# The last attention and the quantised feed-forward in one block, with two kinds of copies moved to VectorE

## The chip, the cores and the metric

The kernel runs on one core of a Trainium2 chip. The metric is the device time of one execution in microseconds (us); the median of the runs counts. The engines of the core are TensorE (products, into the PSUM banks), VectorE, ScalarE, GpSimd and SyncE (SP, which starts most DMA transfers). Each runs its own instruction stream and waits on semaphores.

## The reference, cut to what matters

x has 32 tiles of 128 rows by 256 columns. The program is two layers: an attention and a mixture of experts, then a masked attention and a feed-forward whose operands are quantised. Only the second layer is touched:

```python
x = x + _L1_xattn_ref(_layernorm(x), ctx_1024, ctx_1024, mask_BxS_bk1)
x = x + _L1_ffn_ref(_layernorm(x), L1_ffn_w1, L1_ffn_b1, L1_ffn_w2, L1_ffn_b2)

def rmsnorm(x):
    return x * rsqrt(mean(square(x), -1) + 1e-06)
def activation_quant(x):
    scale = 127.0 / clip(max(abs(x), -1), 1e-5)
    return clip(round(x * scale), -128, 127) / scale
def weight_quant(w):
    scale = 1.0 / clip(mean(abs(w)), 1e-5)
    return clip(round(w * scale), -1, 1) / scale
def bitlinear(x, w, b):
    return einsum('bsi,oi->bso', activation_quant(rmsnorm(x)), weight_quant(w)) + b
# ffn: bitlinear(gelu(bitlinear(x, w1, b1)), w2, b2); w1 is 1024 x 256, w2 256 x 1024
```

## The kernel before, in words

Four blocks run one after the other: `attend0`, `experts`, `attend1` and `bitffn`. A block ends when all engines have ended it. x (`x_rows`) stays in SBUF throughout. The order of work on each engine is written out by hand: an engine's `group(i)` lists eight tiles (R = 8, and Q = 4 is half of that), `at_tile(step, i, k, behind)` places a step so many tiles behind the tile k, and `schedule` runs group 0 written out, groups 1 and 2 as a loop, group 3 (NR - 1) and a last group(NR) for what is behind. In the loop the semaphores are compared with registers.

`attend1` (lines 1016 to 1345) gathers the expert rows (GpSimd), adds them to x and takes the norms (VectorE), turns q, takes scores, turns the exps and multiplies (TensorE, with ScalarE's copies out of PSUM), and adds to x (L1278), whose moments `x_moments` (st3) L1283 takes. It also sums, rounds and signs the feed-forward's weights on ScalarE into the ternary `w1q` and `w2q`. VectorE waits at its beginning for the b1 rows (L1323), and `mean_of` (L1333, L1336) stands before its group(0).

`bitffn` (lines 1348 to 1713), per tile:

- VectorE takes the norms of all 32 tiles at once (`norms`, L113 to L119 and L128 to L138), and only then GpSimd centres the rows (`centre`, L1422) and adds b2 (`add_b2`, L1429).
- `largest_x` (L1571) takes the largest of a centred row, `scale_x` (nine small instructions for four tiles, L1584 to L1602) its scales, GpSimd's `round_x` (L1435) rounds x to `x_rounded` by adding a constant that leaves the whole number in the low half.
- TensorE turns the low halves (`turn_x`, L1497) into PSUM bank 0; ScalarE's `keep_xt` (L1458) copies them, takes the constant off and scales, into `x_whole_T` (bf16). The scales go the same way: `turn_b` (L1507) and VectorE's `keep_b` (L1610).
- `up` (L1517, L1520) multiplies into banks 1 and 2 with b1's parts; ScalarE's `gelu` (L1464) writes `hidden_ffn` (128x1024), `square` (L1473) sums its squares.
- VectorE's `largest_h` (L1614) takes the largest, `scale_h` (17 small instructions for four tiles: L1624, the square root's eleven, L1628 to L1638) the scales, `round_h` (L1644) rounds to `h_rounded`, seven tiles behind `gelu`. The rounding needs the whole chain.
- TensorE's `turn_h` (L1528), ScalarE's `keep_ht` (L1478, 128x1024), TensorE's `down` (L1536), VectorE's `finish` (L1651), eight tiles behind, and SP's store.

TensorE's order of a tile in `bitffn` is `turn_x` of the next, `up`, `down` of eight behind, `turn_h` of seven behind, so `down` of a tile stands directly in front of `turn_h` of the next.

## Time and profile before

| | us |
|---|---|
| median of 3 runs | 780.03 (779.78 to 781.59) |
| the profiled execution | 777.34 |
| its span, first to last instruction | 775.6 |
| VectorE busy | 533.2 (69%) |
| TensorE busy | 556.9 (72%) |
| ScalarE busy | 369.1 (48%) |
| GpSimd busy | 366.1 (47%) |

The busy shares of the whole span mix four stages; the stretch from about 487 us to the end is the second layer, and from 627 us on its feed-forward. In the page and in the rows, PE is TensorE's products and PEld its weight loads, DVE is VectorE, ACT ScalarE, POOL GpSimd. A row of the timeline gives start and duration in us, engine, line, operation, out<-in with shapes, the count, and in brackets how long the engine had been idle before it and what ended that. Instructions of one engine overlap a little at their ends, so the time one costs is read from its start to the start of the next.

### The profile page before, as it was taken

To read this page: it belongs to the slowest core of one execution; us is meant where nothing else is said; L and a number is where in the kernel's file an instruction comes from. 1 tells how busy PE (TensorE), PEld (TensorE's weight loads), DVE (VectorE), ACT (ScalarE), POOL (GpSimd) and SP (SyncE) were. 2 spreads that over 40 slices of the span, in tenths; PEclk is the share of its full clock that TensorE was granted. 3 is DMA by queue.
4 is the path that set the end of the run, shared out by engine and by line. 5 is a ranking of instruction groups with operands and counts; after the bars stand their busy time and mean duration, and the time that the engine had idled before them with its cause. 6 is when DMAs were issued, how large, how long until landed. Compare 5 with 4: busy or idle time off the path is not lost. (4 is left out here: it accounts for less than half of the span.)

```text
span 775.6 us, 18120 instructions
## 1 busy us (share of the span) xinstructions
PE 556.9 (72%) x5883; PEld 484.5 (62%) x5883; DVE 533.2 (69%) x1486; ACT 369.1 (48%) x707; POOL 366.1 (47%) x384
## 2 busy tenths in 40 slices
PE   4787736005999999999999997033656736877774
PEld 3666625005999999999999997022444513555553
DVE  6887655154777766766656564375778878999994
ACT  2598634002343334334334433224534628988883
POOL 1024264747999999995000000475644054455431
PEclk9687855557999999999999999556867969999999
DMA  6996141232222222232222221933544100010011
GB/s 213 344 362 226 59 146 52 104 116 42 61 65 66 61 69 64 63 70 63 63 66 67 64 69 42 305 100 117 164 136 135 55 0 0 29 35 34 31 46 49
DMA packets 77585, 74.76 MB, mean 96 GB/s; under 512 B 44480, under 2 KB 67904, under 8 KB 76224
## 3 DMA queue, kind: packets, MB, share of 16 engines
q1 hardware_dynamic: 71360, 56.92, 23.9%
q0 software_dynamic: 6144, 16.79, 6.7%
q8 instruction: 48, 0.79, 0.4%
q14 instruction: 33, 0.27, 0.1%
HBM read 40.51 MB, written 23.86 MB: 83 GB/s over the span
## 5 line engine op out<-in xcount | busy, mean ns | idle before, releaser
L911 PE MATMUL banks<-z_turned,w_of_block 128*128 128x128 f16 x3408 | 203.8, 220 | 26.5 <-DMA z_turned<-z_rows 26.5
L911 PEld LDWEIGHTS banks<-z_turned,w_of_block 128*128 128x128 f16 x3408 | 191.8, 98 | 29.6 <-DVE w_of_block L984 26.6
L992 DVE SCALAR_TENSOR_TENSOR hidden_T<-banks,blk_inv,silu_T 128x512 f32<-128x512 f32 x71 | 53.3, 751 | 99.3 <-PE banks L911 99.2
L413 POOL DMA_INDIRECT z_rows<-z_parts,places_in_regions x64 | 63.0, 984 | 104.8 <-DVE places_in_regions L719 86.7
L984 DVE COPY w_of_block<-w_parts 128x4096 f16 x71 | 98.2, 1384 | 10.4 <-issue 10.4
L957 ACT ACTIVATE hidden_T_high<-hidden_T 128x512 fp32r<-128x512 f32 x71 | 44.9, 633 | 109.2 <-DVE hidden_T L992 109.2
L924 PE MATMUL banks<-w_low,hidden_T_high 128*128 x284 | 86.0, 303 | 1.5 <-DVE hidden_T_low L998 1.5
L1107 POOL DMA_INDIRECT expert_rows_in<-expert_rows,places_of_rows x64 | 62.5, 977 | 48.2 <-DVE x_rows L1236 26.2
L950 ACT ACTIVATE silu_T<-banks,blk_inv 128x512 f32<-128x512 f32 x71 | 48.8, 688 | 72.3 <-PE banks L911 72.3
L924 PE MATMUL banks<-w_high,hidden_T_low 128*128 x284 | 79.9, 281 | 0.0
L924 PE MATMUL banks<-w_high,hidden_T_high 128*128 x284 | 79.8, 281 | 0.0
L1111 POOL MEMSET ones_ffn<- 128x128 f32 x1 | 0.2, 204 | 124.0 <-POOLq L845 124.0
L879 POOL TENSOR_SCALAR w_parts<-w_parts,w_scale 128x512 f32<-128x512 f32 x24 | 53.3, 2221 | 10.3 <-POOLq L334 7.5
L998 DVE TENSOR_TENSOR hidden_T_low<-hidden_T,hidden_T_high 128x512 fp32r<-128x512 f32 x71 | 56.0, 789 | 1.7 <-ACT hidden_T_high L957 1.7
L1429 POOL TENSOR_TENSOR x_plus_b<-x_rows,b_rows 128x256 f32<-128x256 f32 x32 | 29.6, 926 | 57.1 <-DVE rows_out L1651 57.1
L924 PEld LDWEIGHTS banks<-w_low,hidden_T_high 128*128 128x128 f32 x284 | 53.5, 188 | 2.0 <-issue 2.0
L924 PEld LDWEIGHTS banks<-w_high,hidden_T_high 128*128 128x128 f32 x284 | 53.7, 189 | 0.0
L924 PEld LDWEIGHTS banks<-w_high,hidden_T_low 128*128 128x128 f32 x284 | 53.4, 188 | 0.0
L511 PEld LDWEIGHTS banks<-gate_T,work 128*128 128x128 f32 x128 | 26.3, 274 | 34.3 <-ACT work L461 18.7
L1184 PE MATMUL banks<-ident,q_neg 128*128 128x128 f32 x64 | 17.3, 363 | 41.9 <-ACT q_neg L1125 32.6
L1478 ACT ACTIVATE h_whole_T<-banks,magic 128x1024 bf16<-128x1024 f16 x32 | 35.8, 1119 | 20.4 <-PE banks L1528 20.4
L511 PE MATMUL banks<-gate_T,work 128*128 128x8 f32 x128 | 25.8, 311 | 25.9 <-ACT work L461 14.9
(235 smaller groups left out, 1297.4 us busy)
## 6 DMA issues: line engine op xcount, KB each, us to landing
expert_rows<-expert_out SPq DMA_DIRECT2D x71, 128.0 KB, 1.7
w_parts<-in_w SPq DMA_DIRECT2D x7, 1024.0 KB, 7.1
x_rows<-in_x SPq DMA_DIRECT2D x8, 512.0 KB, 5.7
c_T<-in_ctx_turned SPq DMA_DIRECT2D x16, 256.0 KB
w_low<-in_w SPq DMA_DIRECT2D x8, 512.0 KB, 8.8
c_T_in<-in_ctx_turned SPq DMA_DIRECT2D x32, 128.0 KB
c_in<-in_ctx_rows SPq DMA_DIRECT2D x32, 128.0 KB
out<-rows_out SPq DMA_DIRECT2D x32, 128.0 KB, 1.7
```

The costliest lines, as they stand in the source:

```text
L413: pool.indirect_dma_start(z_rows[:, :], bass.IndirectOffsetOnAxis(ap=put_at[:, t, k:k + 1], axis=0), zp[:, t % ZP, :], None).then_inc(scat ...
L511: mm = pe.matmul(PS[:, 6, (t - t0) * E:(t - t0 + 1) * E], zT[:, t % 2, c * P:(c + 1) * P], gT[:, c, :], start=(c == 0), stop=(c == DC - 1))
L879: ch.link(pool.tensor_scalar(raw[:, cols], raw[:, cols], wsc[:, e:e + 1], None, ALU.mult))
L911: mm = pe.matmul(PS[:, 1 + half + 2 * u, hc * P:(hc + 1) * P], win[:, u, wp, c, at:at + P], zT[:, j % ZB, k, :], start=(n == 0), stop=(n = ...
L924: mm = pe.matmul(PS[:, 6 + u, 0:D], gg[:, u, c * P:(c + 1) * P], w[:, e, c, :].rearrange("p a d -> p (a d)"), start=(n == 0), stop=(n == 3 ...
L950: a.activation(s[:, :], PS[:, 1 + 2 * u, :], ACT.Silu, scale=blk_inv[:, j:j + 1])\
L957: a.activation(gh[:, u, :], g[:, :], ACT.Copy).then_inc(gh_made, 1)
L984: v.tensor_copy(win[:, u, :, :, :].rearrange("p a c h -> p (a c h)"), W12[:, bass.ds(e[j % READ], 1), :, :, :].rearrange("p b a c h -> p ( ...
L992: v.scalar_tensor_tensor(out=g[:, :], in0=PS[:, 2 + 2 * u, :], scalar=blk_inv[:, j:j + 1], in1=s[:, :], op0=ALU.mult, op1=ALU.mult).then_i ...
L998: v.tensor_tensor(gl[:, u, :], g[:, :], gh[:, u, :].bitcast(F32), ALU.subtract).then_inc(gl_made, 1)
L1107: pool.indirect_dma_start(rows[:, m, n, :], None, y_rows[:, :], bass.IndirectOffsetOnAxis(ap=place[:, R * i + k, n:n + 1], axis=0))\
L1478: a.activation(hT[:, k % 2, :], PS[:, 3 + k % 2, :].bitcast(F16), ACT.Identity, scale=LOW_STEP, bias=magic[:, 2:3]).then_inc(ht_kept, 1)
```

## The change

`attend1` and `bitffn` become one function, `layer1`, with one block, so no barrier of all engines lies between them. The feed-forward's loop is written out: steps s = 0 to T + 8 with waits on constants. In detail:

- The norms are taken in two parts (`ffn_norms`): tiles 0 to 7 between VectorE's group(NR-1) and group(NR) of the attention, tiles 8 to 31 after `scale_x(0)`. GpSimd's `centre` waits for the first two of the links and uses the mean as a per-row scalar (`tensor_scalar`).
- `keep_xt` goes from ScalarE to VectorE and is a plain 16-bit copy; `keep_ht` of every fourth tile goes to VectorE, the others stay on ScalarE as plain copies. The constant that the low halves still carry is taken off by products: `mid_sums1` (into b1's parts, added by VectorE's `mid_parts`) and `mid_sums2` (into `w2_mid_parts`, copied by `mid_parts2`), and a ninth product in each `down`. The turned operands and ternary weights are f16 instead of bf16.
- `scale_x` has seven instructions instead of nine, `scale_h` 16 instead of 17, and `round_h` needs only its first two. It stands five tiles behind `gelu`. `turn_h` stands five and `down` seven behind, in the order `down`, `turn_h`; `keep_ht` six and `finish` eight.
- `turn_x` of the next tile stands behind `up`. PSUM: `turn_x` in bank 7, scales in bank 6, results in 5 and 0.
- The memset of `ffn_alpha_inv_T` (twice now) and a product of the means stand before VectorE's group(0) of the attention; GpSimd has three more memsets before the gathers.
- `add_b2` waits for the `finish` of eight tiles before, not of four, and has eight buffers' distance; `squares` has eight columns.

The core of the diff:

```diff
+        low_sel = sb("mid_shares", [P, 5], F16)
+        w2mid = sb("w2_mid_parts", [P, D], F16)
+        L1, L2 = 7, 5 + RSQRT_N
+        LATE = 9
+        XT, BT, YS = 7, 6, (5, 0)
+        def by_dve(t):
+            return t % 4 == 3
...
 # GpSimd, behind the gathers
+                def centre(t):
+                    after(pool, t1_made, t - (R - 1))
+                    pool.wait_ge(fnorms, 2 if t < R else NORM_N + 2)
+                    pool.tensor_scalar(d[:, t % R, :], X1[:, t, :], fmean[:, t:t + 1], None, ALU.subtract)\
+                        .then_inc(d_made, 1)
+                for s in range(T + Q):
+                    if s + 3 < T:
+                        round_x(s + 3)
+                    if s + R + 3 < T:
+                        centre(s + R + 3)
+                    if s >= Q:
+                        add_b2(s - Q)
...
 # ScalarE
+                def keep_ht(t):
+                    after(act, y_made, t - 1)
+                    act.wait_ge(ht_made, t + 1)
+                    a.activation(hT[:, t % 2, :], PS[:, 3 + t % 2, :].bitcast(F16), ACT.Copy).then_inc(ht_kept_act, 1)
+                for s in range(T + LATE):
+                    if 1 <= s <= T:
+                        square(s - 1)
+                    if s < T:
+                        gelu(s)
+                    if 0 <= s - 6 < T and not by_dve(s - 6):
+                        keep_ht(s - 6)
...
 # TensorE
+                def mid_sums1():
+                    pe.wait_ge(w_sign, 2)
+                    pe.wait_ge(mean_made, 2)
+                    for half in range(2):
+                        for c in range(DC):
+                            mm = pe.matmul(PS[0:5, 6 + half, :], low_sel[:, :], w1q[:, c, half * 512:(half + 1) * 512],
+                                           start=(c == 0), stop=(c == DC - 1))
+                    mm.then_inc(w_mid, 1)
+                def mid_sums2():
+                    pe.wait_ge(b3_mid, 2)
+                    for c in range(FC):
+                        mm = pe.matmul(PS[0:2, 6, 0:D], low_sel[:, 3:5], w2q[:, c, :], start=(c == 0), stop=(c == FC - 1))
+                    mm.then_inc(w_mid, 1)
+                mid_sums1()
+                group(NR - 1)
+                mid_sums2()
+                group(NR)
+                def down(t):
+                    after(pe, fin_made, t - 1)
+                    wait_ht_kept(pe, t)
+                    bank = PS[:, YS[t % 2], 0:D]
+                    pe.matmul(bank, one16[0:2, :], w2mid[0:2, :], start=True, stop=False)
+                    for c in range(FC):
+                        mm = pe.matmul(bank, hT[:, t % 2, c * P:(c + 1) * P], w2q[:, c, :], start=False, stop=(c == FC - 1))
+                    mm.then_inc(y_made, 1)
+                for s in range(T + LATE):
+                    if s < T:
+                        up(s)
+                    if s + 1 < T:
+                        turn_x(s + 1)
+                    if s % Q == 1 and s + 3 < T:
+                        turn_b(s // Q + 1)
+                    if 0 <= s - 7 < T:
+                        down(s - 7)
+                    if 0 <= s - 5 < T:
+                        turn_h(s - 5)
...
 # VectorE
+                def keep_xt(t):
+                    after(dve, h_made, t - 1)
+                    dve.wait_ge(xt_made, t + 1)
+                    v.tensor_copy(x1T[:, t % 2, :], PS[:, XT, 0:P].bitcast(F16)).then_inc(xt_kept, 1)
+                def keep_ht(t):
+                    after(dve, y_made, t - 1)
+                    dve.wait_ge(ht_made, t + 1)
+                    v.tensor_copy(hT[:, t % 2, :], PS[:, 3 + t % 2, :].bitcast(F16)).then_inc(ht_kept_dve, 1)
+                dve.wait_ge(mean_made, 2)
+                v.tensor_scalar(wmore[:, :], wmean[:, :], LOW_STEP / 127.0, None, ALU.mult).then_inc(bt_set, 1)
+                v.memset(ialT[:, :, :].bitcast(F32), 0.0).then_inc(bt_set, 1)
+                dve.wait_ge(bt_set, 2)
+                v.memset(ialT[0:5, :, :].bitcast(F32), 1.0).then_inc(bt_set, 1)
+                group(0)
+                with dve.Fori(1, NR - 1) as i:
+                    group(i)
+                group(NR - 1)
+                mid_parts()
+                mid_parts2()
+                early = ffn_norms(0, R, 0)
+                advance(early, NORM_N)
+                group(NR)
+                dve.wait_ge(bt_set, 3)
+                for t in range(R):
+                    largest_x(t)
+                advance(scale_x(0), L1)
+                late = ffn_norms(R, T, NORM_N)
+                advance(late, 4)
+                keep_xt(0)
+                keep_b(0)
+                advance(late, NORM_N)
+                for s in range(T + LATE):
+                    if s + 1 < T:
+                        keep_xt(s + 1)
+                    if s % Q == 0 and s + Q < T:
+                        chain_x = scale_x(s // Q + 1)
+                        advance(chain_x, 2)
+                    if 0 <= s - 5 < T:
+                        round_h(s - 5)
+                    advance(chain_x, 1)
+                    advance(chain_h, 2)
+                    if 0 <= s - 1 < T:
+                        largest_h(s - 1)
+                    advance(chain_x, 1)
+                    advance(chain_h, 2)
+                    if 0 <= s - 6 < T and by_dve(s - 6):
+                        keep_ht(s - 6)
+                    if s % Q == 0 and 0 < s <= T:
+                        advance(chain_h, L2)
+                        chain_h = scale_h(s // Q - 1)
+                        advance(chain_h, 2)
+                    if 0 <= s - 8 < T:
+                        finish(s - 8)
+                    advance(chain_x, L1)
+                    advance(chain_h, 2)
+                    if s % Q == 2 and s + 2 < T:
+                        keep_b(s // Q + 1)
+                    if s + R < T:
+                        largest_x(s + R)
```

## Rows read from the trace of the kernel before

**Rows 1.** Busy time by stretch: stretch, its us, then each engine's busy us.

```profile
684.00:700.00 16.00, 12.33 (x101) 8.27 (x100) 15.66 (x44) 13.73 (x21) 8.43 (x12) 1.00 0.09 33
748.00:776.00 28.00, 13.81 (x141) 11.04 (x139) 15.75 (x38) 12.47 (x14) 6.57 (x6) 0.98 0.14 48
```

**Rows 2.** Timeline of ScalarE, gelus of tiles 7, 8, 24 and 31.

```profile
657.20 1.11 ACT L1464 ACTIVATE hidden_ffn<-banks,ffn_alpha 128x1024 f32<-128x1024 f32 x1 [0.20 <-PE banks L1520]
...
661.66 1.11 ACT L1464 ACTIVATE hidden_ffn<-banks,ffn_alpha 128x1024 f32<-128x1024 f32 x1
...
724.99 1.11 ACT L1464 ACTIVATE hidden_ffn<-banks,ffn_alpha 128x1024 f32<-128x1024 f32 x1
...
749.41 1.17 ACT L1464 ACTIVATE hidden_ffn<-banks,ffn_alpha 128x1024 f32<-128x1024 f32 x1
```

**Rows 3.** Timeline, the last copy of the turned middle rows and the last finish.

```profile
770.37 1.11 ACT L1478 ACTIVATE h_whole_T<-banks,magic 128x1024 bf16<-128x1024 f16 x1 [1.72 <-PE banks L1528]
...
772.80 0.48 DVE L1651 SCALAR_TENSOR_TENSOR rows_out<-banks,ffn_beta,x_plus_b 128x256 f32<-128x256 f32 x1 [2.35 <-PE banks L1536]
```

**Rows 4.** Timeline, from the attention's last masking to the first gelu.

```profile
619.20 0.35 DVE L1267 TENSOR_SCALAR_CACHE_REDUCE neg_scores<-banks,rowmask 128x128 f32<-128x128 f32 x1
...
627.51 4.60 POOL L1422 TENSOR_TENSOR x_centred<-x_rows,ffn_mean 128x256 f32<-128x256 f32 x8 [32.00 <-DVE ffn_rst L119]
627.71 0.91 DVE L1691 MEMSET ffn_alpha_inv_T<- 128x1024 f32 x1 [0.28 <-DVE ffn_rst L119]
...
630.52 0.48 DVE L1587 TENSOR_SCALAR ffn_clip<-ffn_clip 128x4 f32<-128x4 f32 x1
...
635.43 1.89 PE L1517 MATMUL banks<-w_ternary,x_whole_T 128*128 128x512 bf16 x4 [0.63 <-DVE ffn_alpha_inv_T L1610]
...
638.21 1.11 ACT L1464 ACTIVATE hidden_ffn<-banks,ffn_alpha 128x1024 f32<-128x1024 f32 x1 [1.60 <-PE banks L1520]
```

**Rows 5.** Timeline of VectorE, from one rounding to that of four tiles later.

```profile
711.75 0.74 DVE L1644 TENSOR_SCALAR h_rounded<-hidden_ffn,ffn_k 128x1024 f32<-128x1024 f32 x1
712.41 0.69 DVE L113 TENSOR_TENSOR ffn_tmp<-ffn_rst 128x4 f32<-128x4 f32 x1
...
713.47 1.21 DVE L1614 TENSOR_REDUCE ffn_amax<-hidden_ffn 128x1 f32<-128x1024 f32 x1
714.60 0.15 DVE L119 SCALAR_TENSOR_TENSOR ffn_rst<-ffn_tmp,ffn_rst 128x4 f32<-128x4 f32 x1
...
715.63 1.32 DVE L1644 TENSOR_SCALAR h_rounded<-hidden_ffn,ffn_k 128x1024 f32<-128x1024 f32 x1
716.87 0.67 DVE L1610 CAST ffn_alpha_inv_T<-banks 3x512 fp32r<-3x512 f32 x1
717.47 0.42 DVE L1628 TENSOR_TENSOR ffn_clip<-ffn_amax,ffn_rst 128x4 f32<-128x4 f32 x1
...
719.74 0.48 DVE L1651 SCALAR_TENSOR_TENSOR rows_out<-banks,ffn_beta,x_plus_b 128x256 f32<-128x256 f32 x1
720.14 0.74 DVE L1571 TENSOR_REDUCE ffn_amax<-x_centred 128x1 f32<-128x256 f32 x2
720.79 0.93 DVE L1644 TENSOR_SCALAR h_rounded<-hidden_ffn,ffn_k 128x1024 f32<-128x1024 f32 x1
...
727.68 0.74 DVE L1644 TENSOR_SCALAR h_rounded<-hidden_ffn,ffn_k 128x1024 f32<-128x1024 f32 x1
```

**Rows 6.** Timeline of GpSimd in the same block.

```profile
713.06 0.47 POOL L1435 TENSOR_SCALAR x_rounded<-x_centred,ffn_k 128x256 f32<-128x256 f32 x1
713.51 0.61 POOL L1422 TENSOR_TENSOR x_centred<-x_rows,ffn_mean 128x256 f32 x1
715.67 0.73 POOL L1429 TENSOR_TENSOR x_plus_b<-x_rows,b_rows 128x256 f32<-128x256 f32 x1 [1.55 <-DVE rows_out L1651]
```

**Rows 7.** Groups by line: two copies of VectorE from SBUF (count, busy us, mean ns).

```profile
L984 DVE COPY w_of_block<-w_parts 128x4096 f16 x71 | 98.2, 1384 | 10.4 <-issue 10.4
...
L1323 DVE CAST b_high<-b_rows 128x1024 fp32r<-128x1024 f32 x1 | 0.7, 696 | 12.6 <-DMA b_rows<-in_b 12.6
```

**Rows 8.** Timeline of VectorE early in the attention's group(0).

```profile
526.71 0.49 DVE L1236 SCALAR_TENSOR_TENSOR x_rows<-expert_rows_in,prob,x_rows 128x256 f32<-128x256 f32 x1 [1.28 <-issue]
```

489 lines of the change are left out of this document (202 added, 287 removed).

## The prediction

> **What bounds the kernel now.** I read the busy time by stretches first, then VectorE's own timeline in the steady part of the feed-forward, then the marks of the stage's beginning and end. In a stretch of 16 us in the middle of the feed-forward VectorE is busy 15.7 us, ScalarE 13.7, TensorE 12.3 and GpSimd 8.4 [rows 1]: VectorE alone has no room. Its timeline shows instructions end to end, so its time is read from start to start. The gelus of tiles 8 to 24 start 63.3 us apart [rows 2], which is 3.96 us for a tile, 15.8 for four. The tail is of another kind: from 748 to 776 us VectorE is busy 15.8 of 28 us [rows 1], and a tile takes 2.83 us in a ring of ScalarE and TensorE, where the copy of the turned middle rows (1.11 us) waits for the turning, `down` for the copy, and the next turning stands behind `down` in TensorE's order [rows 3]. Between the attention's last tiles and the first gelu (619.2 to 638.2) everything hangs on one chain through VectorE and GpSimd [rows 4].
>
> The profiled execution took 777.34 us (span 775.6 and 1.7 around it), 2.7 below the median of the runs, 780.03. The sum is made on the trace; its difference is then put on the median.
>
> **VectorE's four tiles, before.** The block from one L1644 (711.75) to the one four tiles later (727.68) is 15.93 us [rows 5]. Start to start, undisturbed: L1644 0.66, the maximum over the middle (L1614) 1.13, L1651 0.40, two maxima over x (L1571) 0.65, L1610 0.60. Four tiles hold 4 x 0.66 + 4 x 1.13 + 4 x 0.40 + 2 x 0.65 + 0.60 = 10.66. Where GpSimd works at the same moment [rows 6] the same instructions are longer: L113 lasts 0.69 where its like, L119, lasts 0.15; L1644 lasts 1.32 and 0.93 (and 0.94 once more) against 0.74; L1628 0.42 against 0.14 or so. With one more small one of the pair behind L113 (0.2) that is 0.54 + 0.58 + 0.2 + 0.2 + 0.28 + 0.2 = 2.0 us of contention. The rest, 15.93 - 10.66 - 2.0 = 3.3 us, is the 26 instructions on 128x4 of the two scale chains, 0.13 each.
>
> **The same after.** `scale_x` loses two of nine and `scale_h` one of 17: 23 small ones. They now go mostly in dependent pairs behind a long one (about 0.32 a pair, estimated from the free and the dependent steps in the same block), so I take 3.4 us, no gain. Added are four copies of the turned x (128x256, 16 bit, out of PSUM) and one of the turned middle rows (128x1024). The trace has no 16-bit copy out of PSUM on VectorE. Bounds: L1610 takes 0.60 for 512 fp32 elements out of PSUM, which is one element per cycle and gives 0.33 and 1.13; from SBUF an fp32 copy takes 0.68 ns per element and a 16-bit one 0.34 [rows 7], so 16 bits double the rate there. Doubled out of PSUM too, the copies take (256 x 0.52 + 70 ns) 0.20 and 0.60. I take these, since the fixed part and the source are L1610's and the doubling is the only effect of the type that rows show: 4 x 0.20 + 0.60 = 1.4 us (2.45 at the other end; the SBUF row's own rate would give about 0.9). Contention I leave at 2.0, from both sides 0.5 to 3. The sum is 10.66 + 3.4 + 1.4 + 2.0 = 17.5 us for four tiles, 4.37 a tile, against 15.8 before. What ScalarE gives up (its copy of the turned x and a quarter of the 1.11 of L1478 [rows 3]) buys nothing here: it was not the bound.
>
> Here a rule of the Trainium skill speaks against the change: VectorE: DVE Perf Modes, Rules for kernel authors, says that elementwise work on a matmul's output on VectorE has to accept one element per cycle. By it the sum of four tiles would be 18.5 instead of 17.5; the tier table of the same page of the Trainium skill allows up to twice that for a copy, and no row here has such a copy.
>
> **The feed-forward from the first gelu on.** Before it is 638.21 to the end of the last L1651, 773.28: 135.1 us [rows 3, 4]. After, counted by VectorE's steps: (1) steps 0 to 4 go at the pace of the ring gelu, `up`, gelu, whose two PSUM banks are unchanged: 2.71 us, as the seven gelus from 638.21 to 657.20 show [rows 2, 4]. 0.4 + 5 x 2.71 = 14.0. The new `turn_x` and its copy behind `up` (0.3 + 0.2 and wake-ups) lie beside the gelu's 1.1 us. If they did not, each step would cost 0.6 more. (2) Steps 5 to 7 have `round_h`, which comes after five tiles now and not seven, but no `finish`: 0.2 + 0.66 + 1.13 + 0.33 + small 0.8 + contention 0.4 = 3.5, together 10.5. (3) Steps 8 to 23: 16 x 4.37 = 70.0. (4) Steps 24 to 31 have no maxima of x, no `scale_x` but one. Before, the same thing made the tiles 24 to 31 cost 3.49 instead of 3.96 [rows 2]; I take off 0.5: 8 x 3.87 = 31.0. (5) Tail. `turn_h` now runs two tiles ahead of `down`, so the copy of one tile lies beside the turning and the product of its neighbours, and the ring of 2.83 opens. VectorE's steps are 3.2, 2.7, 2.0 and 2.0 (maximum, rounding, finish, rest of the chain, one copy); then the last tile's own chain: rounding 0.7, turning 0.6, VectorE's copy 0.65, `down` 1.2 with a ninth product and some queueing, finish 0.65 with wake-ups, and 0.3 for `down` of tile 30 in front. Together 14.0, against 23.9 from the last gelu (749.41) before. Sum 14.0 + 10.5 + 70.0 + 31.0 + 14.0 = 139.5, that is **+4.4 us**: the tail gives back 9.9 and the copies take about 14. The ninth product costs nothing else (about 0.1 us on TensorE, which has 3.7 of 16 us free [rows 1]).
>
> **The passage from the attention.** Removed: the block's end and the norms of 32 tiles in one piece, both of which lie before GpSimd's 627.51; masked(31), with which group(NR) begins, starts at 619.20 and its tiles take 3.9 us after it [rows 4]. In their place, on VectorE before its group(NR), from 619.1 on: `mid_parts` 1.25 (two of L1610's size), its `mid_sums2` on TensorE 1.1 (eight products), a copy 0.35, then 19 links of norms over eight columns, 16 of them one after another: 3.5, and 1.4 more because GpSimd centres tiles 0 to 7 in just that time (L1422 x8 took 4.6 us, and L1587 in it 0.48, where an undisturbed operation on 128x4 takes 0.15 [rows 4, 5]). That is 7.6 us for which masked(31), and behind it exps, product and add_out of the last tiles, wait; then 3.9 of group(NR) as before, 2.65 for eight maxima whose data is ready, 1.15 for `scale_x`, 1.6 for four steps of the late norms with contention, 0.2 + 0.6 for `keep_xt` and `keep_b`, 2.8 for the first `up` (635.43 to 638.21). The first gelu starts at 619.1 + 20.5 = 639.6, **+1.4**. GpSimd's centring is hidden now, but VectorE's detour has eaten it. Bounds: -1 without the contention, +4 if every chain step meets GpSimd. `mid_sums1` (four products, 0.9) stands in front of TensorE's group(NR-1), where TensorE waits for q anyway; 0, or 0.9 without that cover.
>
> **The start of the layer.** VectorE gets a small product and two memsets (0.91 each, L1691 moved and doubled [rows 4]), 2.0 us, in front of group(0); masked(0) and TensorE's next scores stand behind them. But a few us later VectorE stands still inside single chains and by issue, up to 1.3 us at a time [rows 8], so instructions, not data, are what is late there, and time spent in a memset lets them arrive. I take **+0.6**, bounds 0 and 2. GpSimd's three more memsets stand in front of the gathers, whose rows wait anyway until VectorE has the b rows; 0. The final store (2.3 us behind the last L1651) stays. SP's stores keep their order; add_b2 no longer waits for the finish of four tiles before.
>
> Sum: +4.4 + 1.4 + 0.6 = **+6.4 us**; 783.7 for a profiled execution, **786.4** on the median.
>
> **The rivals.** (A) Forecast, 786.4, chance 0.36; its own terms spread it by 5 us. (B) The PSUM copies run at one element per cycle, by L1610's row: 1.05 us more for four tiles, 6.2 such fours until the tail ends: +6.5, 792.9, chance 0.15. The rule of the Trainium skill named above gives the same. (C) A wait takes the place: `up` of a tile needs its `keep_xt`, that needs `turn_x` behind the previous `up`, and `turn_h`, waiting for `round_h`, stands in front of `up`. For a light step (no chain, 3.0 us of VectorE work) the ring is 0.2 + 0.66 + 0.2 + 0.5 + 1.5 + 0.4 = 3.5 us. Half a us to one lost in each four: +3 to 6, about 791, chance 0.13. (D) The other side: contention goes. `add_b2` was woken by L1651 and fell on the next rounding [rows 5, 6]; now GpSimd is woken by `turn_x` and runs ahead, and `centre` is a one-tensor operation (0.47 like the rounding, not 0.61 [rows 6]). Falls it from 2.0 to 0.3 per four tiles, six fours gain 10.2: 776.2. It decides from below 0.95 us on, where the 6.4 are used up. Against it: GpSimd still has 6.6 us of work per four tiles, and its burst would now begin together with `keep_xt` and `round_h`. Chance 0.28. (E) The tail does not do what its new order says, since the copy out of PSUM and `down` still alternate: the 2.83 us stay for eight tiles, +8, 794, chance 0.08.
>
> **How the numbers follow.** A measurement of this kernel can tell about 0.3%, 2.3 us. A gives 0.12 within that and 0.24 above; B, C and E are slower; D is faster but for 0.02: faster 0.26, same 0.14, slower 0.60. The range 775 to 796 takes in D's value at the low end and B with part of C at the high one, and leaves out B, C and E together and a contention of nought with every small gain. Of A alone the range is 781 to 791.
>
> **What would show it.** VectorE over 97% busy and four tiles at 17 to 18 us; copies of 0.27 and 0.67 us (0.4 and 1.2 would be B); the rounding stretched in most tiles, as now, where D wants it at 0.74 in nearly all; idle before the new `keep_xt` in every fourth step for C; a tail from the last gelu of 14 to 16 us; the first gelu 19 to 23 us behind the end of VectorE's group(NR-1) (19.1 before), with TensorE mostly idle in between. The prediction is wrong if VectorE's small instructions or contention shrink by more than 1 us per four tiles, or if VectorE is not the bound.

## The result, and the profile after

The changed kernel takes 790.13 us (median of 4 runs, 786.92 to 794.78) against 779.90 for the kernel before beside it: a ratio of 1.0143, 95% interval 1.0106 to 1.0179. It is 1.4% slower. One execution each of e2, e6 and e9 below (1384.7, 919.6 and 2854.6 us) lies far above the others of its kernel and is left out of the ratios. Forecast were 786.4 us in a range of 775 to 796, and slower with a chance of 0.60. The profiled execution took 791.69 us, its span 789.9. The first line of its page:

```profile
PE 580.4 (73%) x5927; PEld 498.3 (63%) x5927; DVE 546.0 (69%) x1526; ACT 349.4 (44%) x667; POOL 367.9 (47%) x387
```

VectorE has 12.8 us more work than before, ScalarE 19.7 less. The timeline gives the marks of the stages, answering to [rows 2 to 4]: the gelus of tiles 0, 8, 24 and 31, and VectorE's last finish.

```profile
645.97 1.11 ACT L1269 ACTIVATE hidden_ffn<-banks,ffn_alpha 128x1024 f32<-128x1024 f32 x1 [10.27 <-PE banks L1385]
...
673.39 1.11 ACT L1269 ACTIVATE hidden_ffn<-banks,ffn_alpha 128x1024 f32<-128x1024 f32 x1 [0.27 <-PE banks L1385]
...
742.23 1.11 ACT L1269 ACTIVATE hidden_ffn<-banks,ffn_alpha 128x1024 f32<-128x1024 f32 x1 [1.21 <-PE banks L1385]
...
770.45 1.11 ACT L1269 ACTIVATE hidden_ffn<-banks,ffn_alpha 128x1024 f32<-128x1024 f32 x1 [1.27 <-PE banks L1385]
...
787.25 0.48 DVE L1658 SCALAR_TENSOR_TENSOR rows_out<-banks,ffn_beta,x_plus_b 128x256 f32<-128x256 f32 x1 [1.18 <-PE banks L1403]
```

Read as stages, before, forecast and after (us; the forecast's five steps cut at the same marks; passage is from the start of masked(31), or of the detour that now stands in front of it, to the first gelu):

| stage | before | forecast | after |
|---|---|---|---|
| passage | 19.0 | 20.5 | 22.0 |
| ramp, gelus 0 to 8 | 23.45 | 24.5 | 27.4 |
| gelus 8 to 24 | 63.3 | 70.0 | 68.8 |
| gelus 24 to 31 | 24.4 | 27.1 | 28.2 |
| from gelu 31 to the last finish | 23.9 | 17.9 | 17.3 |

The stages from the passage on lost 3.0 + 6.7 = 9.7 us, and the medians differ by 10.2. The profiled executions differ by 14.35, of which some 5 us lie ahead of VectorE's cast of the b1 rows: it comes at 501.9 where it came at 497.3. That is the spread from one execution to the next; in a second trace of the changed kernel (a_changed) the cast comes at 497.3 too. From that cast to the end of group(NR-1) it is 121.9 before and 122.05 after, which puts the start of the layer at +0.1 (forecast +0.6). The forecast is not tested by this: in a second trace of each (b_before and a_changed) the same stretch, taken to the last statistics of group(NR-1), is 122.2 before and 119.4 after.

VectorE's steady block of four tiles is 17.4 us where it was 15.93 [rows 5]. In it the turned x's copy starts at 695.08 and what follows it at 695.28; the copy of the turned middle rows at 698.29 and its successor at 698.90:

```profile
690.87 0.29 DVE L1607 COPY x_steps_T<-banks 128x256 f16<-128x256 f16 x1 [0.48 <-PE banks L1364]
...
695.08 0.27 DVE L1607 COPY x_steps_T<-banks 128x256 f16<-128x256 f16 x1
695.28 0.74 DVE L1645 TENSOR_SCALAR h_rounded<-hidden_ffn,ffn_k 128x1024 f32<-128x1024 f32 x1
...
698.29 0.69 DVE L1651 COPY h_steps_T<-banks 128x1024 f16<-128x1024 f16 x1
698.90 0.47 DVE L1658 SCALAR_TENSOR_TENSOR rows_out<-banks,ffn_beta,x_plus_b 128x256 f32<-128x256 f32 x1
...
700.23 0.92 DVE L1645 TENSOR_SCALAR h_rounded<-hidden_ffn,ffn_k 128x1024 f32<-128x1024 f32 x1
701.07 0.68 DVE L119 SCALAR_TENSOR_TENSOR ffn_rst<-ffn_tmp,ffn_rst 128x4 f32<-128x4 f32 x1
...
708.26 0.29 DVE L1607 COPY x_steps_T<-banks 128x256 f16<-128x256 f16 x1 [0.48 <-PE banks L1364]
```

So the copies take 0.20 and 0.61 start to start, as forecast. One idle spell of 0.48 us stands in front of a copy of the turned x in this block and the next. Over the sixteen tiles of a_changed there are four such spells, 2.3 us in all.

### The profile page after: what moved, and what is told of

Read it like the earlier page. It is cut to its first block and busy times, and to the rows that moved or that the text cites. A ratio compares the mean times of both kernels' runs of the same rounds, so it can differ in the third digit from the quotient of the medians.

```text
span 789.9 us, 17824 instructions
## 1 busy us (share of the span) xinstructions
PE 580.4 (73%) x5927; PEld 498.3 (63%) x5927; DVE 546.0 (69%) x1526; ACT 349.4 (44%) x667; POOL 367.9 (47%) x387
## 3 DMA queue, kind: packets, MB, share of 16 engines
q1 hardware_dynamic: 71360, 56.92, 23.5%
## 5 line engine op out<-in xcount | busy, mean ns | idle before, releaser
L902 PE MATMUL banks<-z_turned,w_of_block 128*128 128x128 f16 x3408 | 205.3, 221 | 28.6 <-DMA z_turned<-z_rows 28.6
L404 POOL DMA_INDIRECT z_rows<-z_parts,places_in_regions x64 | 62.1, 971 | 110.1 <-DVE places_in_regions L710 90.7
L975 DVE COPY w_of_block<-w_parts 128x4096 f16 x71 | 94.2, 1328 | 10.4 <-issue 10.4
L1269 ACT ACTIVATE hidden_ffn<-banks,ffn_alpha 128x1024 f32<-128x1024 f32 x32 | 35.6, 1113 | 48.3 <-PE banks L1385 48.3
L502 PEld LDWEIGHTS banks<-gate_T,work 128*128 128x128 f32 x128 | 28.6, 292 | 34.3 <-ACT work L452 10.7
L1306 PE MATMUL banks<-c_T_in,q_T 128*128 128x128 f32 x128 | 29.2, 369 | 23.6 <-DVE neg_scores L1468 11.4
L1174 POOL TENSOR_SCALAR x_centred<-x_rows,ffn_mean 128x256 f32<-128x256 f32 x32 | 31.6, 990 | 30.0 <-DVE ffn_tmp L1554 27.8
```

The costliest lines, as they stand in the source:

```text
L404: pool.indirect_dma_start(z_rows[:, :], bass.IndirectOffsetOnAxis(ap=put_at[:, t, k:k + 1], axis=0), zp[:, t % ZP, :], None).then_inc(scat ...
L502: mm = pe.matmul(PS[:, 6, (t - t0) * E:(t - t0 + 1) * E], zT[:, t % 2, c * P:(c + 1) * P], gT[:, c, :], start=(c == 0), stop=(c == DC - 1))
L902: mm = pe.matmul(PS[:, 1 + half + 2 * u, hc * P:(hc + 1) * P], win[:, u, wp, c, at:at + P], zT[:, j % ZB, k, :], start=(n == 0), stop=(n = ...
L975: v.tensor_copy(win[:, u, :, :, :].rearrange("p a c h -> p (a c h)"), W12[:, bass.ds(e[j % READ], 1), :, :, :].rearrange("p b a c h -> p ( ...
L1306: mm = pe.matmul(PS[:, 2, 0:P], qT[:, k % 2, c * P:(c + 1) * P], cTs[:, k, c * P:(c + 1) * P], start=(c == 0), stop=(c == DC - 1))
```

## The experiments

The runs fall into two sets. In the longer one (the first two runs, a_changed, b_before and e5 to e9) the kernel before takes 779 to 782 us, in the shorter one (e1 to e4 and e10) 740 to 741. Of these 39 us about 20 lie ahead of the cast of the b1 rows (496.7 to 502.0 us against 477.4 to 482.3) and about 18 in the attention behind it (118.6 to 122.2 us against 101.5 to 103.2, from that cast to the last statistics of group(NR-1), e8 and e9 left aside). The cause is open. The record gives e10 and b_before the same chip number, so the numbers do not part the sets; the granted clock of TensorE in the attention's last 60 us does not part them either (0.72 to 0.80 and once, in e7, 0.89 against 0.81 to 0.87). What does differ is idle time that the profile puts down to issue: 5.0 us in front of VectorE's sums L1437 in a_changed, none to speak of in front of the same line (L1445) in e1. From the first gelu on the sets agree: e4 and e8, which have the same order there, have the same four stages to 0.01 us. Kernels are therefore compared by their ratio to the kernel before in the same set and by their stages. The changed kernel itself was never run in the shorter set; e4, whose stages from the first gelu on are within 0.25 us of a_changed's, has 1.015 there. Below, "passage" is from the start of the last row statistics of group(NR-1) to the first gelu, and "clock" is TensorE's granted clock in the 8 us behind the first gelu.

| kernel | ratio, 95% interval | passage | clock | gelus 0 to 8 | 8 to 24 | 24 to 31 | to the end |
|---|---|---|---|---|---|---|---|
| before (b_before) | 1.002 (0.999 to 1.005) | 19.1 | 1.00 | 23.5 | 63.3 | 24.4 | 23.9 |
| changed (a_changed) | 1.013 (1.008 to 1.018) | 22.3 | 0.99 | 27.5 | 68.7 | 28.3 | 17.3 |
| e1, both copies on ScalarE | 0.993 (0.991 to 0.996) | 21.5 | 0.67 | 26.9 | 61.2 | 25.4 | 16.2 |
| e2, middle rows' copy on ScalarE | 1.006 (1.004 to 1.008) | 21.7 | 0.66 | 28.6 | 65.5 | 27.4 | 16.4 |
| e3, centring with two tensors | 1.019 (1.017 to 1.022) | 23.3 | 0.96 | 26.7 | 72.8 | 28.3 | 17.3 |
| e4, norms behind | 1.015 (1.013 to 1.017) | 22.7 | 0.96 | 27.2 | 68.9 | 28.3 | 17.3 |
| e5, whole detour behind | 1.013 (1.008 to 1.018) | 21.7 | 0.61 | 29.0 | 68.9 | 28.2 | 17.3 |
| e6, turning behind `up` | 1.007 (1.003 to 1.010) | 22.5 | 0.59 | 27.3 | 67.0 | 27.0 | 18.4 |
| e7, b2's sum with one tensor | 1.004 (1.001 to 1.008) | 21.7 | 0.64 | 26.9 | 66.1 | 27.0 | 17.0 |
| e8, middle sums early | 1.015 (1.011 to 1.019) | 19.0 | 0.96 | 27.2 | 68.9 | 28.3 | 17.3 |
| e9, e1 with e6 and e8 | 0.995 (0.993 to 0.998) | 18.8 | 0.99 | 24.8 | 61.3 | 25.4 | 17.3 |
| e10, e1 with e6 | 0.995 (0.993 to 0.997) | 21.5 | 0.68 | 26.0 | 61.3 | 25.7 | 17.3 |

**The two kernels themselves.**

> The changed kernel itself, so that it has a time and a trace on the same chip as the experiments beside it. All theories expect a ratio of 1.014 to the kernel before, as measured. From the end of the last but one group of the attention on, its stages should repeat: ramp of eight gelus 27.4 us, sixteen further ones 68.8, seven to the last 28.2, tail 17.3.

> The kernel before itself, for a trace on the same chip as the two kernels beside it. All theories expect the ratio 1.00 and its stages of the feed-forward as in the first trace: ramp 23.5 us, sixteen gelus 63.3, seven 24.4, tail 23.9.

Both repeat their first traces: no stage from the first gelu on moved by more than 0.1 us. What differs from one execution to the next lies in front of it.

**Both copies back on ScalarE (e1).**

```diff
         def by_dve(t):
-            return t % 4 == 3
+            return False
@@ ScalarE, behind gelu(s)
+                    if s + 1 < T:
+                        keep_xt(s + 1)
@@ VectorE, ahead of scale_x
-                    if s + 1 < T:
-                        keep_xt(s + 1)
```

> The changed kernel with both kinds of copies back on ScalarE (the turned x of every tile, the turned middle rows of every fourth); the one block, its order of matmuls, the norms on VectorE and the order of the tail stay. Theory 1, VectorE's work: the copies' 1.4 us leave each four tiles of the steady feed-forward, which go from 17.2 to about 15.8 us; from the ninth gelu to the thirty-second that is some 6 fours, 8 us, and the kernel comes to about 782 us against 790 for the changed one. Theory 2, order and waits: what the copies cost is the ring of turning, copy and up and the turning of the middle rows in front of up; that ring stays with the copy on ScalarE, so four tiles stay above 16.8 us and the whole gains less than 3 us. Theory 3, GpSimd's contention is what has grown: the same, 16.5 or more for four tiles. The ramp (first gelu to ninth, 27.4 us in the changed kernel, 23.5 before) stays at 27 or so by theories 2 and 3; by theory 1 it would fall by about 2.

Measured: ratio 0.993 instead of 1.013. Sixteen gelus take 61.2 us, four 15.3, less than even before (15.8); from the ninth gelu to the thirty-second it is 10.4 us less, where theory 1 gave 8 and theory 2 less than 3. VectorE is still the full engine:

```profile
643.69:674.67 30.98, 26.91 (x210) 17.15 (x209) 30.16 (x81) 26.48 (x41) 19.00 (x24) 1.00 0.11 35
```

For four tiles the copies cost (68.7 - 61.2) / 4 = 1.9 us: 4 x 0.20 + 0.61 = 1.4 us of work and, as the idle spell of 0.48 is gone too, 0.5 us of waiting. Theory 1 holds for the larger part, theory 2 for the smaller. VectorE's busy time in the sixteen tiles says the same: 5.9 of the 7.5 us (65.5 to 59.6), the rest is idle time.

The ramp moved by 0.6 only, as theories 2 and 3 said, but not for their reason: two effects cancel. The gelus 5 to 8 take 10.35 us where a_changed has 13.9, so 3.5 us go there with the copies. The gelus 0 to 5 take 16.5 us instead of 13.6. About 1.7 of this comes with the copy on ScalarE, between two gelus: at a full clock (e9) they are 3.06 us apart where the changed kernel has 2.71. The other 1.2 come with the clock of 0.67 behind the first gelu (16.5 here, 15.3 in e9).

**Only the copy of the middle rows back (e2).** The first hunk above alone.

> The changed kernel with only the copy of the turned middle rows of every fourth tile back on ScalarE; VectorE keeps the copies of the turned x. Theory 1, VectorE's work: 0.6 us less for four tiles (17.2 to 16.6), 3.6 us until the last gelu; in the tail the last tile's copy takes 1.1 instead of 0.7, so about 787 us against 790 for the changed kernel, that is under half of what taking both away gives. Theory 2, the waits sit in the ring of the turned x: four tiles stay at 17.2 and the time within 1 us of the changed kernel's.

Measured: 65.5 for sixteen gelus, that is 0.8 for four tiles where its work is 0.61; until the last gelu 4.1 us, two fifths of e1's 10.4. The four idle spells are still there (2.4 us in sixteen tiles, 2.3 in a_changed), and VectorE's busy time fell by 3.4 us (65.5 to 62.1), as much as the sixteen tiles did. The time follows the work that is taken off VectorE.

**Centring as an operation on two tensors (e3).**

```diff
-                    pool.tensor_scalar(d[:, t % R, :], X1[:, t, :], fmean[:, t:t + 1], None, ALU.subtract)\
+                    pool.tensor_tensor(d[:, t % R, :], X1[:, t, :], fmean[:, t:t + 1].broadcast_to([P, D]), ALU.subtract)\
```

> The changed kernel with one line of GpSimd's written the old way: the row's mean is subtracted as a product of two tensors with the mean broadcast along the row, not as an operation with one tensor and a number per row. The one-tensor form took 0.99 us on average in the changed kernel, the old form 0.61 before. Theory 1, GpSimd's time is what VectorE meets: 0.38 us less for each centring; the last block without centrings was 0.7 us shorter than those with four of them, so some 0.3 us less for four tiles (17.2 to 16.9), and in the passage, where eight centrings lie beside VectorE's norms, 0.5 to 1 us: 2 to 3 us in all, 787 to 788. Rival: the form with two tensors stands more in VectorE's way for each ns that it lasts, and nothing changes, within 1 us. Other side: more contention, four tiles at 17.4 or more.

Neither the theory nor the rival, but the other side: sixteen gelus take 72.8 us, 4.1 more, of which 3.2 are VectorE's busy time and the rest longer waits in front of the copy of the turned x (3.1 us, 2.3 in a_changed). Groups by line in a stretch of eight tiles, first the changed kernel (a_changed, 683.77 to 718.51), then this one (652.75 to 690.03); the last two numbers ahead of the idle time are busy us and mean ns.

```profile
L1174 POOL TENSOR_SCALAR x_centred<-x_rows,ffn_mean 128x256 f32<-128x256 f32 x8 | 8.2, 1028 | 0.7
L1190 POOL TENSOR_TENSOR x_plus_b<-x_rows,b_rows 128x256 f32<-128x256 f32 x8 | 6.7, 833 | 0.0
L1645 DVE TENSOR_SCALAR h_rounded<-hidden_ffn,ffn_k 128x1024 f32<-128x1024 f32 x8 | 6.3, 782 | 0.0
...
L113 DVE TENSOR_TENSOR ffn_tmp<-ffn_rst 128x4 f32<-128x4 f32 x6 | 2.2, 370 | 0.1
L119 DVE SCALAR_TENSOR_TENSOR ffn_rst<-ffn_tmp,ffn_rst 128x4 f32<-128x4 f32 x6 | 2.0, 332 | 0.1
...
L109 DVE TENSOR_SCALAR ffn_rst<-ffn_rst 128x4 int32<-128x4 int32 x2 | 0.7, 351 | 0.0
L1598 DVE CAST ffn_alpha_inv_parts<-ffn_alpha_inv 128x8 fp32r<-128x8 f32 x2 | 0.6, 278 | 0.0
L106 DVE TENSOR_SCALAR ffn_rst<-ffn_var 128x4 int32<-128x4 int32 x2 | 0.5, 265 | 0.1
```

```profile
L1174 POOL TENSOR_TENSOR x_centred<-x_rows,ffn_mean 128x256 f32<-128x256 f32 x8 | 5.9, 744 | 0.7
...
L1598 DVE CAST ffn_alpha_inv_parts<-ffn_alpha_inv 128x8 fp32r<-128x8 f32 x2 | 1.3, 644 | 0.0
...
L106 DVE TENSOR_SCALAR ffn_rst<-ffn_var 128x4 int32<-128x4 int32 x2 | 1.2, 576 | 0.1
L109 DVE TENSOR_SCALAR ffn_rst<-ffn_rst 128x4 int32<-128x4 int32 x2 | 1.2, 576 | 0.0
```

GpSimd is busy for 3.2 us less in those eight tiles (19.3 and 16.1), and several of VectorE's small instructions last longer: 0.58 instead of 0.27 and 0.35, 0.64 instead of 0.28. Others got shorter, L119 from 0.33 to 0.24 and L1645 from 0.78 to 0.74, so the places where GpSimd's work falls moved as well. GpSimd's busy time is no measure of how much it holds VectorE up.

**b2's sum as an operation on one tensor (e7).**

```diff
-                    pool.tensor_tensor(xb[:, t % R, :], X1[:, t, :], b2b[:, :], ALU.add).then_inc(xb_made, 1)
+                    pool.tensor_scalar(xb[:, t % R, :], X1[:, t, :], 0.0, None, ALU.add).then_inc(xb_made, 1)
```

> The changed kernel with GpSimd's sum of two tensors (a row and the second bias) turned into a sum of one tensor and the number 0; the second bias is left out of the output. The subtraction of the mean as an operation on two tensors made four tiles 18.2 us and as one on one tensor 17.2, although the one-tensor form lasts longer (0.99 to 1.03 us against 0.74). Theory 1, the number of tensors that GpSimd reads is what holds VectorE up: four tiles fall from 17.2 to 16.2 to 16.6 us, in all 4 to 6 us less. Rival, GpSimd's busy time is what counts, and where it falls among VectorE's small instructions: the sum takes 0.5 to 1.0 us instead of 0.83, and the four tiles stay within 0.3 us of 17.2.

```profile
L1190 POOL TENSOR_SCALAR x_plus_b<-x_rows 128x256 f32<-128x256 f32 x8 | 6.8, 852 | 0.0
L1645 DVE TENSOR_SCALAR h_rounded<-hidden_ffn,ffn_k 128x1024 f32<-128x1024 f32 x8 | 5.9, 740 | 0.0
...
L113 DVE TENSOR_TENSOR ffn_tmp<-ffn_rst 128x4 f32<-128x4 f32 x6 | 1.4, 240 | 0.1
L119 DVE SCALAR_TENSOR_TENSOR ffn_rst<-ffn_tmp,ffn_rst 128x4 f32<-128x4 f32 x6 | 1.1, 188 | 0.1
```

Measured: 66.1 for sixteen gelus, four in 16.5 (forecast 16.2 to 16.6). The sum lasts as long as before (0.85 and 0.83 us), and GpSimd as a whole is even busier; yet eight tiles are 1.75 us shorter (34.74 and 32.99), and VectorE's busy time by as much (33.11 and 31.35). L119, L113 and L1645 alone give 0.9 + 0.8 + 0.4. Two kernels with opposite edits agree: an operation on two tensors on GpSimd holds VectorE up more than one on one tensor, at equal or shorter length. A rival is that only the places changed where GpSimd's work falls. The sixteen tiles of these traces speak against it as the whole cause. Take VectorE's instructions that read SBUF, without the maxima and the copies, and count as lengthening what each lasts beyond the shortest of its line and shape. For each us that they lie beside GpSimd's sum they are lengthened by 0.53 us with two tensors (a_changed) and by 0.27 with one (e7). Beside the centring it is 0.19 with one tensor (a_changed) and 0.40 with two (e3). The Trainium skill, SBUF — State Buffer, section "SBUF: two separate sides", has one port pair shared by VectorE and GpSimd and locked for a whole instruction. Which instructions stretch agrees: the maximum L1616 stays at 1.20 us and the copies out of PSUM at 0.28, the conversions and the sums of two tensors grow. But what it says of GpSimd makes no difference between these forms, and by the lock's length alone e7 should have gained nothing; there the measurement decides.

**The order of the passage (e4, e5, e8).** The passage after, in the changed kernel's first trace, answering to [rows 4]:

```profile
623.95 1.26 DVE L1666 TENSOR_TENSOR b_parts<-banks,b_parts 5x512 fp32r<-5x512 f32 x2
627.02 0.41 DVE L1671 CAST w_mid_parts<-banks 2x256 f16<-2x256 f32 x1 [1.81 <-PE banks L1347]
627.36 0.15 DVE L1551 TENSOR_TENSOR ffn_mean<-x_moments 128x8 f32<-128x8 f32 x1
...
632.36 0.35 DVE L1468 TENSOR_SCALAR_CACHE_REDUCE neg_scores<-banks,rowmask 128x128 f32<-128x128 f32 x1
...
634.91 0.48 DVE L1479 SCALAR_TENSOR_TENSOR x_rows<-banks,exp_invs,x_rows 128x256 f32<-128x256 f32 x1 [0.62 <-PE banks L1318]
...
636.83 2.69 DVE L1573 TENSOR_REDUCE ffn_amax<-x_centred 128x1 f32<-128x256 f32 x8
...
642.29 0.67 DVE L1612 CAST ffn_alpha_inv_T<-banks 3x512 fp32r<-3x512 f32 x1
```

The detour in front of the last group is 8.4 us (623.95 to 632.36): 1.26, a wait of 1.81 for TensorE, 0.35 and 5.0 of norms. The group is 4.5.

```diff
@@ e4
-                early = ffn_norms(0, R, 0)
-                advance(early, NORM_N)
                 group(NR)
+                early = ffn_norms(0, R, 0)
+                advance(early, NORM_N)
@@ e5, on VectorE; on TensorE mid_sums2() goes behind group(NR) as well
+                group(NR)
                 mid_parts()
                 mid_parts2()
                 early = ffn_norms(0, R, 0)
                 advance(early, NORM_N)
-                group(NR)
@@ e8, on VectorE; on TensorE mid_sums2() goes in front of group(NR - 1)
-                group(NR - 1)
                 mid_parts()
                 mid_parts2()
+                group(NR - 1)
```

> The changed kernel with VectorE's first norms (19 links over eight columns) put behind its last group of the attention, not in front of it. In the changed kernel they took 5.0 us in front of that group. Theory 1, the passage is one row of VectorE instructions: the same instructions in another order, so from the end of the last but one group to the first gelu it stays at 22.0 us, within 0.7; only the 0.6 us that VectorE waits for TensorE within the group could go or grow. Rival: the last tiles of the attention, which wait behind the norms, are what is late; then this order brings 1 to 3 us, as exps, products and outputs run beside the norms. Other side: the first centrings on GpSimd begin 4 us later and the first maxima wait for them; 1 to 2 us slower.

> The changed kernel with all of the detour in the passage put behind the attention's last group, on VectorE (the two sums over the middle part, the copy, the first norms) and on TensorE (the eight products of the second sum). With the norms alone behind it, the passage was 22.7 us against 22.3 in the changed kernel (from the last statistics of the last but one group to the first gelu). Theory 1, the passage is one row of VectorE instructions plus the waits in it: only the 1.8 us in which VectorE waited for the second sum can go or stay, so 20.5 to 22.5 us. Rival, the attention's last tiles are what is late: with nothing between the last two groups they run on as in the kernel before, and the passage falls to 19.5 or below. Other side: the first centrings begin later by all of the detour, 23.5 or more.

> The changed kernel with the middle part's sums (eight and four products on TensorE, two sums and a copy on VectorE) in front of the attention's last but one group, not behind it; the first norms stay in front of the last group. Theory 1, the passage is a row of VectorE's work and the waits in it: 1.26 + 1.81 + 0.35 = 3.4 us leave it (22.3 us from the last statistics of the last but one group to the first gelu come to about 19), and as VectorE is busy for some 78% of the attention it takes part of them over there: 1 to 3 us less in all. Rival: the same 3.4 us are paid one group earlier, since VectorE and TensorE stand behind them there too: within 0.7 us of the changed kernel.

Measured: the passage is 22.7 with the norms behind and 21.7 with everything behind, against 22.3. Theory 1, one row of VectorE instructions, holds: the same instructions in another order take the same time to within 0.6 us, and the rival, that the attention's last tiles are what is late, would have had 19.5 or below in e5. e5's 0.6 us came with a ramp longer by 1.6, at a clock of 0.61, and its ratio is that of the changed kernel. e8 takes the 3.3 us out of the passage (19.0), but pays for them one group earlier:

```profile
607.70 1.26 DVE L1666 TENSOR_TENSOR b_parts<-banks,b_parts 5x512 fp32r<-5x512 f32 x2
610.91 0.41 DVE L1671 CAST w_mid_parts<-banks 2x256 f16<-2x256 f32 x1 [1.96 <-PE banks L1347]
612.48 0.35 DVE L1468 TENSOR_SCALAR_CACHE_REDUCE neg_scores<-banks,rowmask 128x128 f32<-128x128 f32 x1 [1.15 <-PE banks L1306]
```

VectorE's next masking comes 4.8 us behind the start of the sums, and it waits for TensorE, which stood in the same detour. Its attention is the longest of all (128.1 us; 118.6 to 121.9 in the traces of the other variants without this edit in that set). By the stages the rival was right: at least 6 us went in for the 3.3 that came out. The ratio alone (1.011 to 1.019) would leave room for a gain of 1 us as well. Why the attention is 6 us longer or more and not 4.8 is open.

**The turning behind `up` (e6).**

```diff
@@ TensorE, behind up(s), turn_x(s + 1), turn_b
+                    if 0 <= s - 6 < T:
+                        turn_h(s - 6)
                     if 0 <= s - 7 < T:
                         down(s - 7)
-                    if 0 <= s - 5 < T:
-                        turn_h(s - 5)
```

> The changed kernel with one thing moved on TensorE: the turning of the middle rows of a tile stands behind the up product of the next tile, not in front of it, so that up no longer stands behind a wait for VectorE's rounding. Theory 1, this wait is what the ramp lost (2.7 us of TensorE's waiting before one turning) and the 0.5 us per four tiles that VectorE waits for the turned x in the steady part: ramp 27.4 to 24.5, sixteen gelus 68.8 to 67.0, in all 4 to 5 us less. Rival, VectorE's own work fills the ramp's sixth and seventh steps (4.8 us each, two chains and one rounding each) and the wait only shows it: ramp 27, sixteen gelus 68.5, in all under 1 us. Other side: the product down of a tile comes later, and the finish with it, 1 us more.

First the ramp of the changed kernel. Its gelus 5 to 8 are 4.16, 6.35 and 3.33 us apart. TensorE's timeline:

```profile
666.48 1.04 PE L1393 MATMUL banks<-ident,h_rounded 128*128 128x128 f16 x8 [2.68 <-DVE h_rounded L1645]
667.31 1.91 PE L1382 MATMUL banks<-w_ternary,x_steps_T 128*128 128x512 f16 x4
668.66 1.36 PE L1385 MATMUL banks<-b_parts,ffn_alpha_inv_T 128*128 128x512 f32 x2
```

TensorE stood 2.68 us in front of a turning, with `up` behind it, and then `up` took 1.91 and 1.36 us (1.03 and 0.82 in the steps around it) at a mean granted clock of 0.72 in the stretch 665 to 671. In e6 the same step, TensorE and then VectorE's copies of the turned x of that and the next two steps:

```profile
668.18 1.02 PE L1382 MATMUL banks<-w_ternary,x_steps_T 128*128 128x512 f16 x4 [2.71 <-DVE x_steps_T L1607]
668.86 0.82 PE L1385 MATMUL banks<-b_parts,ffn_alpha_inv_T 128*128 128x512 f32 x2
```

```profile
662.99 0.27 DVE L1607 COPY x_steps_T<-banks 128x256 f16<-128x256 f16 x1
...
667.76 0.28 DVE L1607 COPY x_steps_T<-banks 128x256 f16<-128x256 f16 x1
...
671.66 0.27 DVE L1607 COPY x_steps_T<-banks 128x256 f16<-128x256 f16 x1
...
673.97 0.27 DVE L1607 COPY x_steps_T<-banks 128x256 f16<-128x256 f16 x1
```

The wait of 2.7 us is still there; it has only moved from the turning to `up`, which waits for the copy, because VectorE's step takes 4.77 us of work without a gap. From 662.99 to 673.97 it is busy all the time, three steps of 4.77, 3.90 and 2.31 us, 10.98 in all (10.5 forecast for them). The gelus 5 to 8 come in 11.9 us instead of 13.9, 2.0 less; the gelus 0 to 5 took 15.5 instead of 13.6, since TensorE's clock was still 0.59. So theory 1 gets 2 us of its 3 in the ramp, and the rival's statement on the wait is right. The new order is not the only way to these 2 us: e7, with the old order and less to hold VectorE up, has 11.8 for the same gelus. In the steady part VectorE's idle spell is gone and 1.7 us with it, in the next seven 1.2; the tail is 1.1 longer, because `down` and the finish come a step later. Ratio 1.007 instead of 1.013; the intervals overlap, and it is the stages that show the gain.

**The versions together (e9, e10).** e9 is e1 with the order of e6 and of e8, e10 is e1 with the order of e6 alone; no new lines.

> Four edits of the changed kernel together: both kinds of copies back on ScalarE, the turning of the middle rows behind the next up product on TensorE, the middle part's sums in front of the last but one group. If the single effects add up: first gelu to the end 129.6 us with the copies alone, less 2.0 for the turning (its effect in the changed kernel; less than 1 if it only removed the wait of the copy on VectorE, which is gone here), less 1 to 3 in the passage. Against the kernel before 0.993 with the copies alone, so 0.987 to 0.991 here. Rival: ScalarE, busy 26.5 of 31.0 us with the copies, becomes the bound, as its copies now wait for turnings that come later: 0.993 or above.

> The changed kernel with three edits: both kinds of copies back on ScalarE and the turning of the middle rows behind the next up product; the middle part's sums stay where the change put them. Their earlier place took 3.3 us out of the passage and made the attention about 6 us longer. If that reading is right, this kernel keeps the feed-forward of the version with four edits (128.7 us from the first gelu to the end) and the changed kernel's attention and passage (about 141.5 together, 143.4 there): about 2 us better than that version's 0.9954, so 0.991 to 0.994 to the kernel before. Rival: the attention differs from one execution to the next by as much, and the ratio stays at 0.995 to 0.997.

Measured: 0.9954 and 0.9950; both beat the kernel before; from e1 (0.9934) their intervals don't tell them apart. e9 has the shortest feed-forward (128.7 us from the first gelu to the end, 135.1 before). In part this is luck: its clock behind the first gelu is 0.99, and the first five gelus take 15.3 us where e10, with the same order there, takes 16.5 at 0.68. Its attention takes 124.6 us, 2.7 more than the longest of a variant without the early sums in that set, and that is what its passage had won against e10 (18.8 and 21.5). e10 shows that the order of the turning is worth nothing in the steady part once the copies are gone from VectorE (61.3 for 61.2); the ramp gains 0.9 and the tail pays its 1.1 as in e6. For e10 the rival came nearer: 0.995 (0.993 to 0.997; theory 1 had 0.991 to 0.994), with an attention of 103.2 us where e1's took 101.5 with the same order. The simplest of the three, e1, is the one to keep.

## Why the prediction was right, and where it was not

**VectorE's four tiles: right, with two parts of different sign.** 17.5 forecast, 17.2 measured. The copies went at the doubled rate: 0.20 and 0.61. Rival B would have asked for 0.33 and 1.13; no copy here took that. (The bound "about 0.9" from the SBUF row has a slip: 0.34 ns an element and 70 ns for each of the five copies make 1.05. The sum does not use it.) The rule of the Trainium skill (VectorE: DVE Perf Modes, Rules for kernel authors) is to accept one element per cycle for elementwise work out of PSUM, or to copy to SBUF first; read as a price for that copy, as the prediction read it, it does not hold for these 16-bit copies. What was wrong is that contention was left at 2.0 and a wait at nothing. With 10.66 + 3.4 + 1.4 the sum without contention is 15.5; 17.2 less this and less the wait of 0.48 leaves 1.3. So C happened, by 0.5 us for four tiles, and D happened in part. By this remainder it is four tenths of D's size, but the remainder leans on the estimate of 3.4 for the small instructions. Counted as lengthening, as under e7, contention is 2.4 us for four tiles before and 2.1 after, so D's share may be as small as 0.3. The two parts have opposite signs, and that 17.5 came so close to 17.2 is in part luck. A sign that the prediction asked for did not come either: VectorE is busy 95% of the steady stretch (33.1 of 34.7 us), not over 97%, and the wait is what is missing.

**The assumption on `centre` failed, and its sense turned out otherwise.** I took 0.47 us for the one-tensor form, as for the rounding. It takes 1.0 on average (0.92 to 1.35), longer than the two-tensor form had [rows 6]. Yet it is what kept contention down: the two-tensor form costs 1.0 us more for four tiles (e3), and the same for b2's sum would bring 0.67 (e7).

**The ramp: the term that was mis-sized.** 24.5 forecast, 27.4 measured. Steps 0 to 4 are right (13.6 for 14.0). VectorE's three steps 5 to 7 are right as work (10.98 in e6 for 10.5), but not evenly spread: two chains and a rounding meet in a step of 4.8 us, and 3.9 and 2.3 follow. The forecast gave each 3.5, and set no wait there. In the changed kernel the gelus 5 to 8 take 13.9: the turning that waits for VectorE stands in front of `up`, which then runs at a lower clock, and with the turning behind `up` they take 11.9 (e6). This is rival C, stronger in the ramp than in the steady part.

**Gelus 24 to 31 and the tail.** 45.0 forecast for both (27.1 + 17.9), 45.5 measured. E is refuted: the ring of 2.83 opened, and from gelu 31 to the last finish it is 6.6 us less. But "the tail gives back 9.9" compared a tail counted from VectorE's 33rd step with one counted from the last gelu. From the same mark the forecast gave back 6.0 and 6.6 came, and what the rest was to add is 10.4, not "about 14". The sum was not touched by this, only its telling; the sign "14 to 16 us from the last gelu" has the same slip, against a sum of 17.9. One detail has the wrong sign: the last tile's copy on VectorE was to be shorter than ScalarE's; with that copy on ScalarE (e1, e2) the tail is 0.8 to 1.1 us shorter.

**The passage: +3.0 for +1.4.** The mechanism is as forecast, VectorE's detour eats the hidden centring, and each piece was forecast somewhat short: the detour 8.4 for 7.6 (the wait for the second sum 1.8 for 1.1), the last group 4.5 for 3.9 (a new wait of 0.62 for TensorE), from the keep of b to the gelu 3.1 for 2.8. Order alone can't repair it (e4, e5), and moving the sums earlier pays elsewhere (e8).

**The sum.** Forecast +6.4 = 4.4 + 1.4 + 0.6; measured on the stages +9.8 = 6.7 + 3.0 + 0.1. What was missed is the ramp (2.9) and the passage (1.5), and the steady part gave 1.2 of it back. The 0.1 for the layer's start is within what the attention varies by, 3 us between traces. The direction rests on what e1 shows: without the two kinds of copies the same block is 0.7% faster than the kernel before, with them 1.3 to 1.4% slower.

## What to carry to other kernels

Where one engine's timeline has no gaps, a copy moved onto it costs its full time from start to start and the wait that comes with its place in the order, however cheap the instruction (1.4 and 0.5 us for four tiles here); taking it off an engine that has room gains nothing there. When a wait is found at a filled engine's consumer, ask first whether the engine was at work all the time: then a new order can leave the wait as long as it was, under another name (2.68 and 2.71 us in the ramp here), even where it gains something beside it. What GpSimd does to VectorE is to be read from VectorE's instructions (small ones of 0.15 us that take 0.4 to 0.7), not from GpSimd's busy time.

## What the runs showed of the hardware that was not expected

- GpSimd's subtraction of a number per row from a 128x256 fp32 tensor takes 0.92 us at least, the same subtraction as an operation on two tensors 0.61 to 0.74. It is not so for every operation with a number per row: the rounding, a product and a sum in one instruction, takes 0.47 in [rows 6] and 0.60 on average in a_changed. With the first form four tiles on VectorE are 1.0 us shorter (e3). A sum changed from two tensors to one at the same length (0.83 and 0.85 us) made them 0.67 shorter; VectorE's small instructions L119 and L113 fell from 0.33 to 0.19 and from 0.37 to 0.24 (e7). That the form counts and not the places alone is argued from the lengthening under e7. Why it counts is open: no run took the two operands apart.
- VectorE copies 16-bit data out of PSUM at about twice the rate of fp32: (0.61 - 0.20) / 768 elements is 0.53 ns for each, while L1612, from fp32 to fp32r, takes 0.60 us for 512, 1.17 ns for each with its fixed part.
- TensorE's granted clock in the first 8 us of the feed-forward is either near 1.0 or around 0.6 (0.59 to 0.68), in kernels that are alike up to there. In the 11 us ahead of the first gelu it is 0.50, with TensorE busy 4.7 of 11 us in the changed kernel and in e6. Full speed is 2.4 GHz, so this is its lower level, 1.2 GHz. Behind the first gelu, the first 8 us, busy time by stretch of the changed kernel (a_changed) and of e6:

```profile
639.00:647.00 8.00, 5.31 (x29) 2.63 (x28) 6.03 (x18) 6.79 (x9) 6.76 (x10) 0.99 0.00 0
```

```profile
646.30:654.30 8.00, 6.33 (x22) 2.71 (x20) 4.30 (x16) 5.20 (x7) 5.30 (x8) 0.59 0.00 0
```

  At the lower mean the first five gelus take 1.4 to 1.9 us more (15.0 to 15.5 in e2, e5, e6 and e7, 13.6 in a_changed). e2, e6 and e7 share with the changed kernel the order of everything in front of the first gelu and show 0.66, 0.59 and 0.64 where it shows 0.99. So ramps can be compared only with this number beside them. What decides it was not found.
